# Both 1024-row matrices times M3 by seven products of half blocks; table rows stored unsplit; the adapters' chunks in another order

## The chip, the cores and the metric

One Trainium2 chip; the kernel uses one of its NeuronCores. The metric is the device time of a run in microseconds. The time before is 886.78 us, the median of 3 runs (886.35 to 887.19).

## The reference, cut to what matters

`x` is 64 x 64 x 1024: 4096 rows of 1024 numbers, 32 tiles of 128 rows, two batches of 64 rows to a tile. Four residual layers follow one another:

```
x = x + base0(x) + 2 * sum_e gate[e] * (x A0[e]^T) B0[e]^T   # 1024x1024 weight, router over 8 experts, rank 16, top 2
x = x + W1[condition[b]]^T x[b]                              # mixes the 64 rows of a batch
x = x + (x B2[id]^T) A2[id]^T                                # 64 second adapters, rank 16, one per batch
x = x + x W3^T + b3 + 2 * (x A3[id]) B3[id]                  # 1024x1024 weight, 32 third adapters, rank 16
```

Everything is float32. The kernel multiplies the weight matrices with each other first. With M0 = I + W0^T and M3 = I + W3^T it makes M0 M3, B0 M3, U2 M3 (U2: all 64 second adapters' output matrices as 1024 rows), and M0 and B0 times the second adapters' 1024 and the third adapters' 512 input columns. A tile then needs one pass over these products. Each float32 product is made as three matmuls of a rounded part (`_hi`) and a rest (`_lo`): hi x hi, lo x hi, hi x lo (`PASSES`).

## The kernel before

**Setup** is a list of groups, `GROUPS`, of a chunk (512 columns of the right-hand side, in `mov`) and a block (128 rows of the left-hand side, in `stat`). A group is 8 x 3 = 24 matmuls into one of four banks (`product`, L1484). There are 27 groups of the three chunks with adapters' columns (chunks 0 and 1: second adapters; chunk 2: third adapters; blocks: eight of M0 and B0) and 34 of the two chunks of M3 (eight blocks of U2, B0, eight of M0): 61 groups, 1464 matmuls of 512 columns. A block is loaded by SyncE three groups ahead, gets its piece of the identity from GpSimd (`stat_identity`), its rounded part from ScalarE (`stat_hi`) and its rest from VectorE (`stat_lo`, L1094 is the helper `rest`). The next chunk is loaded and split one piece a group. Each group's result is evicted by ScalarE (`group_hi`) and VectorE (`group_lo`) as rounded part and rest. Those of the D chunks go to a stage in memory of the core and from there to the tables `t2` and `t3` in DRAM (`store_md`), whose rows hold rounded part, rest and the adapter's own matrix, 416 columns. Those of U2 go to the table `tu2` (`store_u2`), those of M0 M3 stay as weights: the plain columns in `w`, and B11, B21, B22 and the sums T1 to T4 for the products of the tiles.

**The tiles** are worked in 16 pairs (`fore`, `step`, `last`); for each pair a 1024 x 832 part of the product is already made by seven products P1 to P7 of half blocks, from the pair's rows and their sums (`sums`, on GpSimd). For each tile SyncE loads the chosen table rows (`load_md`), GpSimd puts them into `w` and `b03` (`place_w`, L707, two casts; `place_b`), ScalarE and GpSimd split the adapters' own matrices (`ud_hi`, `ud_lo`), and TensorE makes the plain product (`plain`, L1513), the hidden product (L1562), the gate's transpose, the experts (L1528), the mixing (L1534) and the ranks (L1556). Each engine's order is written out by hand; engines wait for each other by semaphores. All DMAs are issued by SyncE on one queue, in program order. The load for the next tile waits until GpSimd has placed the one before.

The time of the seam matters here: in the kernel before, `store_md` of the last D chunk lies some 30 groups ahead of the first `load_md`.

## Time and profile before

| | |
|---|---|
| median of 3 runs | 886.78 us |
| span of the profiled execution (the profile gives no time of its own beside it) | 884.5 us |
| TensorE busy | 876.8 us, 99% |
| VectorE busy | 651.4 us, 74% |
| ScalarE busy | 350.5 us, 40% |
| GpSimd busy | 241.3 us, 27% |
| DMA | 187.71 MB, 212 GB/s |

Busy time counts an instruction from its start to its end. Matmuls overlap, so the rate of TensorE is read from the starts in the chain, not from the mean length. A line such as L1094 is a helper's: operations are told apart by the names of what they write.

### The profile page before, as it was taken

The numbers are of one execution on the slowest core, as the hardware profiler recorded it, in microseconds if no ns is written. First come the engines' busy times: TensorE is split into PE (matmuls) and PEld (weight loads), VectorE is DVE, ScalarE is ACT, GpSimd is POOL, SyncE is SP. The second block draws the span as 40 slices with busy tenths as digits, with TensorE's granted clock in tenths as the row PEclk, the third lists the DMA queues.
The fourth block names the chain that finished last, engine by engine and source line by source line (L and its number), as shares of the span: only waits on it lengthen the run. The fifth ranks groups of instructions, "written<-read, shape, count | busy, mean of one in ns | idle before, by whom it ended". The sixth has DMA issues, their size and how long they took to land.

```text
span 884.5 us, 15284 instructions
## 1 busy us (share of the span) xinstructions
PE 876.8 (99%) x4668; PEld 810.8 (92%) x4668; DVE 651.4 (74%) x1865; ACT 350.5 (40%) x800; POOL 241.3 (27%) x379
## 2 busy tenths in 40 slices
PE   8999999999999999999999999999999999999997
PEld 7888888888888889999999999999999999999997
DVE  6555444444358634798998899898899899899896
ACT  5544333333334423434434434434334344345333
POOL 1100010010000004415415425325325335235230
PEclk9999999999999999999999999999999999999999
DMA  7978686899663575566666667667667667566674
GB/s 243 311 265 282 207 262 211 284 350 274 191 193 126 162 222 174 164 179 200 213 185 216 202 182 230 196 188 222 192 188 230 185 195 224 186 195 215 196 205 144
DMA packets 105606, 187.71 MB, mean 212 GB/s; under 512 B 20022, under 2 KB 66870, under 8 KB 105526
## 3 DMA queue, kind: packets, MB, share of 16 engines
q1 hardware_dynamic: 105526, 186.76, 68.3%
q8 instruction: 37, 0.61, 0.3%
q14 instruction: 43, 0.35, 0.1%
HBM read 143.20 MB, written 49.81 MB: 218 GB/s over the span
## 4 chain that ended last, share of the span: by engine, by line
PE 96%; DMA 1%; DVE 1%; POOL 1%; SPq 0%; issue 0%; ACT 0%; DVEq 0%; POOLq 0%
PE ps_o L1487 28%; PE ps_w L1521 16%; PE ps_d L1513 15%; PE ps_d L1521 12%; PE ps_s L1487 9%; PE ps_o L1534 5%; PE ps_d L1528 4%; PE ps_o L1556 3%; PE ps_s L1562 1%; PE ps_w L1528 1%; DMA chunk_a_raw<-mov 1%; DMA stat_raw<-x 1%; PE ps_s L1568 0%; PE ps_o L1589 0%; DVE outb L1333 0%
## 5 line engine op out<-in xcount | busy, mean ns | idle before, releaser
L1094 DVE TENSOR_TENSOR stat_lo<-stat_raw,stat_hi 128x1024 fp32r<-128x1024 f32 (+1 forms) x127 | 152.2, 1199 | 22.2 <-ACT stat_hi L798 19.8
L798 ACT ACTIVATE stat_hi<-stat_raw 128x1024 fp32r<-128x1024 f32 (+1 forms) x127 | 116.7, 931 | 12.1 <-POOL stat_raw L682 5.4
L1513 PE MATMUL ps_d<-w_hi,stat_hi 128*128 128x392 f32 x256 | 86.9, 340 | 0.3 <-POOL w_lo L707 0.3
L1513 PE MATMUL ps_d<-w_hi,stat_lo 128*128 128x392 f32 x256 | 86.8, 339 | 0.0
L1513 PE MATMUL ps_d<-w_lo,stat_hi 128*128 128x392 f32 x256 | 86.8, 339 | 0.0
L1487 PE MATMUL ps_o<-chunk_a_hi,stat_hi 128*128 128x512 f32 x216 | 84.3, 390 | 0.9 <-DVE chunk_a_lo L1094 0.9
L1487 PE MATMUL ps_o<-chunk_a_lo,stat_hi 128*128 128x512 f32 x216 | 84.1, 389 | 0.0
L1487 PE MATMUL ps_o<-chunk_a_hi,stat_lo 128*128 128x512 f32 x216 | 84.0, 389 | 0.0
L707 POOL CAST w_hi<-mdraw 128x512 fp32r<-128x512 f32 x32 | 31.3, 977 | 157.0 <-DMA mdraw<-t 156.9
L682 POOL TENSOR_TENSOR stat_raw<-stat_raw,ident 128x128 f32<-128x128 f32 x40 | 20.5, 514 | 186.5 <-DMA stat_raw<-stat 186.5
L1487 PE MATMUL ps_o<-chunk_b_hi,stat_hi 128*128 128x512 f32 x152 | 59.1, 389 | 0.0
L1487 PE MATMUL ps_o<-chunk_b_hi,stat_lo 128*128 128x512 f32 x152 | 59.1, 389 | 0.0
L1487 PE MATMUL ps_o<-chunk_b_lo,stat_hi 128*128 128x512 f32 x152 | 59.1, 389 | 0.0
L1487 PEld LDWEIGHTS ps_o<-chunk_a_hi,stat_hi 128*128 128x128 f32 x216 | 40.5, 188 | 9.9 <-DVE chunk_a_lo L1094 1.5
L1513 PEld LDWEIGHTS ps_d<-w_hi,stat_hi 128*128 128x128 f32 x256 | 48.0, 188 | 0.7 <-issue 0.6
L1487 PEld LDWEIGHTS ps_o<-chunk_a_lo,stat_hi 128*128 128x128 f32 x216 | 40.5, 188 | 8.5
L1487 PEld LDWEIGHTS ps_o<-chunk_a_hi,stat_lo 128*128 128x128 f32 x216 | 40.6, 188 | 8.3
L1513 PEld LDWEIGHTS ps_d<-w_hi,stat_lo 128*128 128x128 f32 x256 | 48.0, 188 | 0.1
L798 ACT ACTIVATE y_hi<-y_raw 128x416 fp32r<-128x416 f32 x48 | 26.4, 550 | 54.8 <-DVE y_raw L1362 48.3
L1513 PEld LDWEIGHTS ps_d<-w_lo,stat_hi 128*128 128x128 f32 x256 | 48.0, 188 | 0.0
L743 POOL TENSOR_TENSOR rows_raw<-rows_raw,stat_raw 128x512 f32<-128x512 f32 x32 | 46.4, 1451 | 2.3
L1521 PE MATMUL ps_w<-T_hi,stat_hi 128*128 128x416 f32 x128 | 46.4, 363 | 0.1
(230 smaller groups left out, 2346.4 us busy)
## 6 DMA issues: line engine op xcount, KB each, us to landing
up<-tu SPq DMA_DIRECT2D x124, 256.0 KB, 4.6
stat_raw<-stat SPq DMA_DIRECT2D x59, 512.0 KB, 4.2
mdraw<-t SPq DMA_DIRECT2D x128, 208.0 KB, 3.2
stat_raw<-x SPq DMA_DIRECT2D x32, 512.0 KB, 3.4
out<-outb SPq DMA_DIRECT2D x30, 512.0 KB, 5.5
t<-md_a SPq DMA_DIRECT2D x16, 576.0 KB, 5.4
rows_raw<-x SPq DMA_DIRECT2D x32, 256.0 KB, 3.7
chunk_a_raw<-mov SPq DMA_DIRECT2D x24, 256.0 KB, 5.5
```

Source lines behind the costliest of these rows:

```text
L682: nc.gpsimd.tensor_tensor(out=raw[:, s, :], in0=raw[:, s, :], in1=ident[:, :], op=ALU.add).then_inc(pool_stat, 1)
L707: last = nc.gpsimd.tensor_copy(w[part][:, :, MD_AT:P_AT].rearrange("p k (q r) -> p k q r", r=RANK), rows.rearrange("p q (k r) -> p k q r", ...
L743: nc.gpsimd.tensor_tensor(out=dst, in0=in0, in1=in1, op=op).then_inc(pool_s, 1)
L798: return nc.scalar.activation(dst, src, ACT.Copy)
L1094: return nc.vector.tensor_tensor(out=dst, in0=src, in1=rounded.bitcast(F32), op=ALU.subtract)
L1487: last = nc.tensor.matmul(ps_g[g % BANKS][:, :], st[g % RING][a][:, k, :], mchunk[c % 2][v][:, k, :], start=k == 0 and m == 0, stop=k == K ...
L1513: last = nc.tensor.matmul(plain_bank(t)[:, 0:WCOLS], rows[a][:, k, :], w[c][:, k, :], start=k == 0 and m == 0, stop=k == KB - 1 and m == l ...
L1521: last = nc.tensor.matmul(ps[:, 0:SH], rows[a][:, k, :], weights[c][:, k, :], start=first and k == 0 and m == 0, stop=k == HALF_KB - 1 and ...
L1528: last = nc.tensor.matmul(ps, hgT[t % 2][a][:, :], b03[c][:, cols], start=first and m == 0, stop=m == len(PASSES) - 1, skip_group_check=True)
L1534: last = nc.tensor.matmul(out_bank(turn, n)[:, 0:OW[n]], mix[turn % 2][a][:, :], y[t % 2][c][:, Y[n]], start=first and m == 0, stop=m == l ...
L1556: return nc.tensor.matmul(out_bank(turn, n)[:, OK[n]], stackT[:, :], up[:, OX[n]], start=first, stop=True, skip_group_check=True)
L1562: last = nc.tensor.matmul(ps_ud, d3m[:, k, :, :, :].rearrange("p h b r -> p (h b r)"), u2s[:, k, :, :, :].rearrange("p h b r -> p (h b r)" ...
```

## The change

- The 27 D groups come in the order chunk 2, 0, 1. The first chunk (third adapters) is worked at the start; chunks 0 and 1 (second adapters) at the end of setup.
- Between them, M0 and U2 times M3 are made in 8 units (`unit`), each two blocks (s and s+4) by all 1024 columns, with seven products of 12 matmuls and sums of half blocks, of quarters of M3 and of outputs. The order in a unit is P1, P5, P6, P3, P7, P2, P4, in three banks, with two sets of banks. B0 times M3 stays at 48 matmuls.
- The sums of M3's quarters and their splits are made beside the first chunk (`m3_lo`, `m3_hi`, `m3_t3`, at groups 3, 4, 6 and 7).
- The tables' rows are stored in float32, unsplit: B0's 16 columns by a DMA of their own (`store_mb`), 272 columns a row. `place_w` and `place_b` make rounded part and rest from them: a cast and a subtraction on GpSimd.
- The first pair has an order of its own (`first`): P1 and P2 ahead of the first plain product, P6 ahead of the second.
- T1 to T4 are made of unsplit sums in four operations and split at the end of setup (`t_sum`, `final_hi`, `final_lo`). Several semaphores are merged.

The diff, cut to its core:

```diff
-    GROUPS = [(c, s) for c in D_CHUNKS for s in M0_FIRST + [B0_BLOCK]]
-    GROUPS += [(3, s) for s in U2_BLOCKS + [B0_BLOCK] + M0_BLOCKS]
-    GROUPS += [(4, s) for s in M0_BY_TWO + U2_BLOCKS + [B0_BLOCK]]
+    GROUPS = [(c, s) for c in (2, 0, 1) for s in M0_FIRST + [B0_BLOCK]]
+    PREPARED = {3: 0, 4: 1, 6: 2, 7: 3}
...
+            def m3_lo(k):
+                dve.wait_ge(pool_m3, m3_adds(k))
+                dve.wait_ge(ld_m3[k], 64)
+                subtract(CT1raw[:, k, :], CT4raw[:, k, :], C3raw[:, k, :]).then_inc(dve_m3sum, 1)
+                dve.wait_ge(dve_m3sum, 4 * k + 1)
+                subtract(CT2raw[:, k, :], CT3raw[:, k, :], CT1raw[:, k, :]).then_inc(dve_m3sum, 1)
+                dve.wait_ge(act_m3, PRODUCTS * k + 4)
+                rest(CB22[lo][:, k, :], CT3raw[:, k, :], CB22[hi][:, k, :]).then_inc(dve_m3sum, 1)
+                rest(CB11[lo][:, k, :], C3raw[:, k, :], CB11[hi][:, k, :])
+                dve.wait_ge(dve_m3sum, 4 * k + 2)
+                rest(CT1[lo][:, k, :], CT1raw[:, k, :], CT1[hi][:, k, :])
+                dve.wait_ge(pool_t3, k + 1)
+                subtract(CT4raw[:, k, :], C3raw[:, HALF_KB + k, :], CT2raw[:, k, :]).then_inc(dve_m3sum, 1)
...
+            for g in range(EACH):
+                if g + 2 < EACH:
                     stat_lo(g + 2)
+                if g in PREPARED:
+                    m3_lo(PREPARED[g])
+            a_sums(0)
+            for which in range(PRODUCTS):
+                a_lo(0, which)
+
+            def unit(u):
+                more, rows = u + 1 < UNITS, u >= M0_UNITS
+                if not more:
+                    stat_lo(B0_NUMBER)
+                out_sum(u, C12)
+                if rows:
+                    row_lo(u, C12)
+                out_sum(u, C22)
+                if more:
+                    a_sums(u + 1)
+                    a_lo(u + 1, A11_AT)
+                    a_lo(u + 1, S1_AT)
+                if rows:
+                    row_lo(u, C22)
+                out_sum(u, C11)
...
+            def quarter(ps, rows, weights, first):
+                for k in range(HALF_KB):
+                    for m, (a, v) in enumerate(PASSES):
+                        last = nc.tensor.matmul(ps[:, :], rows[a][:, k, :], weights[v][:, k, :], start=first and k == 0 and m == 0,
...
+                quarter(W, a_parts(u, A11_AT), CB11, True).then_inc(pe_prod, 1)
+                pe.wait_ge(dve_a, done(u, P5))
...
+                quarter(Y, a_parts(u, S1_AT), CT1, True).then_inc(pe_prod, 1)
+                pe.wait_ge(dve_a, done(u, P6))
+                pe.wait_ge(act_wpart, 3 * u + 1)
+                quarter(W, a_parts(u, S2_AT), CT2, False).then_inc(pe_prod, 1)
...
+                pe.wait_ge(dve_csum, summed(u, C22))
+                quarter(W, a_parts(u, A22_AT), CT4, False).then_inc(pe_prod, 1)
...
+            def store_mb(c):
+                sp.wait_ge(act_ev, made(c))
+                table, first = table_rows(c)
+                sp.dma_start(table[first:first + PER, :, B0_COLS].rearrange("a p f -> p a f"), md_b0[c][:, :, :]).then_inc(st_mb, 16)
...
+                if g == G - 1:
+                    for n in range(STORES):
+                        store_md(1, n)
+
+            sp.wait_ge(ld_ids, 16 * 4)
+            choose(0)
             choose(1)
+            store_mb(1)
+            load_s2(0)
+            for made_c in D_CHUNKS:
+                sp.wait_ge(st_md[made_c], 16 * STORES)
+            sp.wait_ge(st_own, 16 * OWN_STORES)
+            load_md_first(slice(0, MAIN_COLS.stop), ld_md)
             load_s3(0)
             load_s4(0)
+            sp.wait_ge(st_mb, 16 * len(D_CHUNKS))
+            load_md_first(B0_COLS, ld_mb)
...
+                rows = mdraw[:, :, MAIN_COLS].rearrange("p q (k r) -> p k q r", r=RANK)
+                upper_w, lower_w = [v[:, :, MD_AT:P_AT].rearrange("p k (q r) -> p k q r", r=RANK) for v in w]
+                nc.gpsimd.tensor_copy(upper_w, rows).then_inc(pool_md, 1)
+                pool.wait_ge(pool_md, 2 * t + 1)
+                nc.gpsimd.tensor_tensor(out=lower_w, in0=rows, in1=upper_w.bitcast(F32), op=ALU.subtract).then_inc(pool_md, 1)
...
+            def first():
+                a, b = 0, 1
+                pe.wait_ge(dve_x0, 1)
+                pe.wait_ge(dve_final, 4 + len(FINALS))
+                pe.wait_ge(dve_set, SETS)
+                pe.wait_ge(act_ev, G)
+                winograd(ps_w, A11, B11, True).then_inc(pe_p[0], 1)
+                pe.wait_ge(dve_b0, 1)
+                winograd(ps_x, A12, B21, True).then_inc(pe_p[1], 1)
+                pe.wait_ge(act_b0, 2)
+                pe.wait_ge(pool_md, 2 * a + 2)
+                plain(a, range(KB)).then_inc(pe_hl, 1)
+                hidden_product(a)
+                pe.wait_ge(act_part, 1)
+                pe.wait_ge(dve_s, s_order(0).index(1) + 1)
+                winograd(ps_w, S[1], T2, False).then_inc(pe_p[5], 1)
+                pe.wait_ge(dve_x1, 1)
+                pe.wait_ge(pool_md, 2 * b + 2)
+                plain(b, range(KB)).then_inc(pe_hl, 1)
```

## Rows read from the trace of the kernel before

**Rows 1.** The page: its first line and the busy times.
```profile
span 884.5 us, 15284 instructions
PE 876.8 (99%) x4668; PEld 810.8 (92%) x4668; DVE 651.4 (74%) x1865; ACT 350.5 (40%) x800; POOL 241.3 (27%) x379
```

**Rows 2.** Waits of TensorE: for whom, us in total, times, longest.
```profile
PE ps_w L1482 <- POOL ident L665: 1.5, 1, 1.5
PE ps_o L1487 <- DVE chunk_a_lo L1094: 0.9, 1, 0.9
...
PE ps_d L1513 <- POOL w_lo L707: 0.3, 1, 0.3
```

**Rows 3.** Chain that ended last, setup: start, length in us, what.
```profile
29.96 16.32 PE ps_o L1487 x72
...
329.16 5.45 PE ps_s L1487 x24
```

**Rows 4.** Stretches: us, each engine's busy us, granted clock, DMA share, GB/s.
```profile
9.16:57.20 48.04, 48.04 (x211) 39.63 (x212) 31.50 (x44) 24.93 (x39) 5.54 (x10) 1.00 0.81 280
155.00:247.00 92.00, 92.00 (x408) 76.17 (x407) 39.48 (x51) 32.37 (x51) 7.87 (x17) 1.00 0.89 275
449.00:817.00 368.00, 367.91 (x2171) 363.37 (x2171) 332.93 (x1141) 149.83 (x405) 148.92 (x220) 1.00 0.67 203
880.00:884.50 4.50, 0.48 (x3) 0.14 (x2) 1.81 (x4) 0.00 (x0) 0.00 (x0) 0.83 0.64 233
```

**Rows 5.** Groups by form: count, busy us, mean ns, idle before.
```profile
L1094 DVE TENSOR_TENSOR rows_lo<-rows_raw,rows_hi 128x512 fp32r<-128x512 f32 x40 | 27.6, 689 | 18.9 <-ACT rows_hi L798 18.4
L743 POOL TENSOR_TENSOR stat_raw<-stat_raw 128x512 f32<-128x512 f32 x32 | 41.6, 1300 | 4.9 <-DMA stat_raw<-x 3.5 <-PE ps_o L1487 1.4
```

**Rows 6.** VectorE in order of time, setup and loop: start, length in us.
```profile
28.91 0.69 DVE L1094 TENSOR_TENSOR rows_lo<-rows_raw,rows_hi 128x512 fp32r<-128x512 f32 x1
29.52 0.68 DVE L1094 TENSOR_TENSOR md_a<-ps_o,md_a 128x512 fp32r<-128x512 f32 x1
30.12 1.22 DVE L1094 TENSOR_TENSOR stat_lo<-stat_raw,stat_hi 128x1024 fp32r<-128x1024 f32 x1
...
541.34 2.31 DVE L1094 TENSOR_TENSOR stat_lo<-stat_raw,stat_hi 128x1024 fp32r<-128x1024 f32 x1
```

**Rows 7.** TensorE in order of time, the warm-up, early and late.
```profile
2.12 1.70 PE L1482 MATMUL ps_w<-ident 128*128 128x128 f32 x7
...
4.68 2.00 PE L1482 MATMUL ps_w<-ident 128*128 128x128 f32 x12
```

**Rows 8.** DMA packets of two stretches: 215 to 216 us, 212.5 to 213.
```profile
DMA packets 664, 0.34 MB, mean 339 GB/s; under 512 B 1, under 2 KB 664, under 8 KB 664
...
DMA packets 488, 0.10 MB, mean 194 GB/s; under 512 B 385, under 2 KB 479, under 8 KB 488
```

**Rows 9.** SyncE in order of time: DMA issues of 1024 packets each.
```profile
207.90 2.50 SPq L587 DMA_DIRECT2D w_raw<-wr  x1
...
212.26 0.57 SPq L448 DMA_DIRECT2D t<-u2k  x1
```

**Rows 10.** The page's DMA issues: count, KB each, median us to landing.
```profile
mdraw<-t SPq DMA_DIRECT2D x128, 208.0 KB, 3.2
```

**Rows 11.** GpSimd in order of time, the second tile's rest of a pair.
```profile
544.07 0.61 POOL L707 CAST w_lo<-mdraw 128x512 fp32r<-128x512 f32 x1
```

**Rows 12.** Chain that ended last, first pair and a later one.
```profile
354.24 2.27 PE ps_w L1521 x12
...
357.43 0.44 PE ps_s L1562 x8
...
360.21 1.14 PE ps_d L1521 x6
...
548.48 4.26 PE ps_d L1513 x24
```

More of the change, by code:

```diff
@@ L387, in build, with summed @@
         pe_out = [sem(f"pe_out{n}") for n in range(3)]
+        C12, C22, C11, C21 = range(4)
+        def summed(u, which):
+            return 3 * u + which + 1
         CONSTS = 6
@@ new lines, in load_a @@
+            def load_a(u, at):
+                n = u * PRODUCTS + at
+                if n >= SPOTS:
+                    sp.wait_ge(pe_prod, n - SPOTS + 1)
+                else:
+                    sp.wait_ge(pe_group, max(g for g in range(EACH) if g % RING == spot(u, at) // 2) + 1)
+                if u > 0 and at in (A11_AT, A12_AT, A22_AT):
+                    sp.wait_ge(ld_a[at], 16 * u)
+                first = (M0_BLOCKS if u < M0_UNITS else U2_BLOCKS)[0] + u % HALF_KB
+                block = first if at in (A11_AT, S4_AT, A12_AT) else first + HALF_KB
+                columns = upper if at in (A11_AT, S1_AT) else lower
+                sp.dma_start(araw(u, at), stat[block][:, columns, :]).then_inc(ld_a[at], 16)
@@ L656, in last @@
                 sp.wait_ge(st_last, 16 * 6)
-            pairs(step)
+            pairs(first, step)
             last(PAIRS - 1)
@@ L790, in last @@
                 mix_identity(TURN_A)
-            pairs(step)
+            pairs(first, step)
             last(PAIRS - 1)
@@ L1086, in last @@
                 h3T_last(TURN_A)
-            pairs(step)
+            pairs(first, step)
             last(PAIRS - 1)
@@ new lines, in _ @@
+            for u in range(UNITS):
+                unit(u)
+            b0_upper, b0_lower = [[v[:, half, :] for v in st[B0_NUMBER % RING]] for half in (upper, lower)]
+            pe.wait_ge(dve_stat, stats(B0_NUMBER))
+            pe.wait_ge(dve_row, 4 * (UNITS - 2 - M0_UNITS) + C21 + 1)
+            quarter(ps_u[0][0], b0_upper, CB11, True).then_inc(pe_b0, 1)
+            pe.wait_ge(dve_csum, summed(UNITS - 2, C11))
+            quarter(ps_u[0][1], b0_upper, CT1, True).then_inc(pe_b0, 1)
+            pe.wait_ge(act_b0, 1)
```

1454 lines of the change are left out of this document (928 added, 526 removed).

## The prediction

> **What bounds the kernel now.** I read the page first: TensorE is busy for 876.8 of 884.5 us, VectorE for 651.4 [rows 1]. Then the waits of TensorE: the longest are 1.5 us before the warm-up, 0.9 us for the first chunk and 0.3 us at the first tile [rows 2]. Third, the chain that ended last: from 9.16 us on it is one unbroken series of matmuls, three groups of 24 in 16.32 us, a fourth in 5.45, that is 0.2267 us from matmul to matmul and 5.44 us a group of 512 columns (the mean of 389 ns a matmul overlaps the next one and must not be summed) [rows 3]. So a setup matmul that is left out is worth 0.2267 us exactly as long as nothing else is late. Last, the stretches: in setup VectorE is busy 43 to 66% and the DMA engines 81 to 89%, in the loop over tiles VectorE 90% [rows 4]. There is room, but the question of this case is latency at the seams, and there are two new ones.
>
> **Part 1, the products.** Before, both 1024-row matrices times M3 take 16 blocks x 2 chunks x 24 = 768 matmuls. After, 8 units of 7 products of 12 make 672. The 48 of B0 and the 648 with the adapters' chunks stay. 96 x 0.2267 = **21.8 us removed**.
>
> **Part 2, inside a unit (19.04 us, a product 2.72).** VectorE makes 4 sums and 7 low parts, in the units of the second adapters also 3 outputs and 4 low parts: 18 operations of 0.6 us from start to start (0.69 each) [rows 5, 6], about 12 us. The tight order is at the end: the output C22 waits for product 5 (13.6 us into the unit), then come 4 sums, each on the one before, at 0.73, and one low part: 13.8 + 0.6 + 2.9 + 0.7 = 18.0, and the next unit wants it at 19.04. ScalarE copies the first product out of its bank some 4 us into the next unit, wanted at 5.44. Loads are issued a product or more ahead; 22 issues at 0.47 make 10 of 19 us on the queue. I take 0; bounds 0 and 1 us in each of 7 units. B0 and the chunk after it: eight chunk pieces are loaded two products ahead and split during B0's 10.9 us, 0.
>
> **Part 3, the seam into the units.** While the first chunk is used (nine groups, it ends at 57.2), VectorE gets 4 preparations of M3, 10 operations each, beside the splits of the stationary blocks. The sixth block can be split from about 26.3 to 27.4 (its load waits for group 1, ScalarE first evicts group 2, which ends at 24.5). Then: 4 x 6.7 (10 starts at 0.6 plus two dependent steps and the wait on GpSimd's 1.3 us subtraction), 3 splits of 1024 columns at 1.14, four dependent sums 2.9, one low part 0.7: 27.4 + 26.8 + 3.4 + 3.6 = about 61.4 to 61.8. TensorE stands for **4.6 us**. From below: 2 if the first preparation slips ahead. From above: a VectorE operation beside GpSimd's stretches (2.31 against 1.23 us for 1024 columns) [rows 6]; of each preparation 1.3 us lie beside GpSimd, half of it lost: +0.65 x 4 = 2.6, so 7.2.
> A wait this long may let the clock fall. At the very end, after its last matmul at about 880.3, the granted clock of the stretch is 0.83 [rows 4], so it fell from 2.4 to 1.2 GHz within 4.2 us of idling, and in the warm-up 7 matmuls took 1.70 us and later 12 took 2.00 [rows 7]. If the first product behind the wait runs at half, it costs 2.7; I take **0.9** between 0 and 2.7. The Trainium skill, "TensorE: Matmul & The Clock Gate", Part 1, has the same two levels and says that an idle array falls back to the lower; by that rule the whole product is paid and the sum is 1.8 us worse.
>
> **Part 4, the seam into the tiles.** Before, the second adapters' and third adapters' tables lay in memory long before; the first tile's rows were loaded inside setup and TensorE waited 0.3 us. Now the last chunk of setup is the second adapters', so its table is stored, loaded and split after the last group. With T the end of that group:
> - The stores of 2 MB wait for the eviction of the last group but one (T-4.7), 8 issues at 0.47. 4096 packets of 512 B; a stretch that is nothing but such packets moved 664 in 1 us [rows 8], so 6.2 us: drained at T+2.7.
> - The 16 columns of B0 go as 4096 packets of 64 B, behind them in the queue, after T+0.8. Small packets: 488 in 0.5 us, 385 of them under 512 B [rows 8], so 16 engines handle them in 16 ns or less; 4096 take 2.9 to 4.2 us. The issue itself can block: 1024 packets of 32 B held the queue's issuer for 2.50 us where 1024 of 512 B held it for 0.57 [rows 9]. T+5.7.
> - x's half block and four loads of 128 KB, 2 us, and the rest of the landing: T+9 (a table row takes 3.2 us from issue to landing, median) [rows 10].
> - GpSimd: a cast and now a subtraction of 512 columns, 0.6 + 1.3 [rows 5, 11]: placed at T+11.
> - Then, in GpSimd's order, two sums 2.6, two small splits 1.5, B0's columns 0.5; only then may the second tile's four loads be issued (1.9) and land (2.8), and be placed (1.9): T+22.2.
> Until the second tile's plain product TensorE has P1, P2, the plain product, the hidden product and P6: 2.27 + 2.27 + 4.26 + 0.44 + 2.27 = 11.5 us [rows 12]. **10.7 us** idle; a lower clock in the first wait is swallowed by the second. Bounds: 7 (packets and landings at their best) and 21 (below).
> - Behind it only P7, the experts and the hidden product stand before T1 (3.7 us, before also P6: 6.0 from 354.24 to 360.21) [rows 12], and the exponential of the second gate is now queued behind the eviction that waits for the experts. Experts at +2.9, exponential +3.3, rest of the gate 1.8, low part 0.4: +5.7. **2.0 us**, bounds 0 and 3. The 0.3 of before goes.
> The Trainium skill, "DMA: Bandwidth & Descriptors", Specifications, speaks against this edit: below 512 B a transfer is a read-modify-write and off line rate. The 32 B packets of the trace went faster by the packet than the 512 B ones, but they went into SBUF; no row shows 64 B written to memory. What slow small packets would do here is rival D, priced from rows.
>
> **Part 5, the loop over tiles.** A table row shrinks from 208 to 136 KB. On GpSimd the cast of the low part (0.6) becomes a subtraction (1.3), 0.8 us a tile with B0's, 32 times, 25 us on an engine that is busy 40%. Hidden: the second tile's place ends at 544.7, the product that wants it starts at 548.48, 3.8 us later [rows 11, 12]. The next on that queue, ScalarE's h2, moves by 0.8 where VectorE takes it up 1.1 us later. 0; if the cover were gone 0.3 x 15 pairs. 27 low parts of D groups leave VectorE in setup, off the path. The merged semaphores cost 0.
>
> **Sum.** -21.8 + 4.6 + 0.9 + 10.7 + 2.0 - 0.3 = -3.9 us: span 880.6. The page gives the profiled execution's span only, 884.5; the median 886.78 lies 2.3 above, so 882.9; I forecast **883.1 us**, 0.4% less.
>
> **Rivals.** (B) The seams are shorter: first wait 2, no clock loss, last seam 7, gate 0: -21.8 + 9 - 0.3 = -13; I price it half way, 877. For it: each bound was stacked on a worst order. Against: the chain of part 4 has ten steps that can't overlap.
> (C) VectorE and GpSimd hinder each other in the preparation of M3, and the clock's product is paid whole: +2.6 + 1.8: 887.5, no change. For it: the 2.31 us row.
> (D) Slower: the 64 B packets decide. Place: the queue between the second adapters' table and the first tile. Price: at the issuer's pace of [rows 9], 2.50 us for 1024, the store takes 10.0 us in place of 2.9, +7.1; the same store in unit 0 (behind it the sixth block of unit 1, and in ScalarE's order behind that the first product's bank) adds 2: 892.2. It turns the sign from a store of 7 us on (+3.9) and shows as slower from 8.4 us. For it: the issuer's row. Against: the mixed stretch of [rows 8], and that the issuer may only have waited for room.
> (E) The last 1 us of a unit isn't there: each unit is late by 1, 7 us: 890. Against: 0.6 a start is the most regular row.
> That the change would not leave matmuls out is no rival: the count is written in its loops.
>
> **How the numbers follow.** Forecast 0.42 (its own range 880 to 886), B 0.20, C 0.14, D 0.14, E 0.10. A change within 0.2%, 1.8 us, can't be told from none. Faster: B and most of the forecast's case, 0.56. Same: 0.04 of the forecast, C, together 0.17. Slower: D, E and a tail of the forecast's, 0.27. Range 876.5 to 891: it leaves out the far end of B and the upper part of D.
>
> **What would show it.** Of the matmuls of 128x512, 1368 instead of 1464. Idle TensorE in three places: before the first product of unit 0 (4 to 6 us, released by VectorE's low part), before the first plain product and before the second (5 and 5, GpSimd's w_lo), before T1 of the first pair (2, VectorE's y_lo). No waits at all in units 1 to 7 and in the later pairs. Wrong if TensorE waits inside the units, if the loop over tiles gets longer than 33.5 us a pair, or if the store of B0's columns takes over 6 us.

## The result, and the profile after

The changed kernel takes 907.44 us (median of 4 runs, 905.93 to 908.36), the kernel before 886.57 beside it (4 runs): ratio 1.0232, 95% interval 1.0218 to 1.0247. It is 2.3% slower. The forecast was 883.1 us and its range ended at 891.

The page's first line and busy times [answers to rows 1]:

```profile
span 905.7 us, 15339 instructions
PE 867.2 (96%) x4572; PEld 797.5 (88%) x4572; DVE 682.5 (75%) x1896; ACT 368.2 (41%) x827; POOL 289.5 (32%) x379
```

TensorE has 96 matmuls less, as written, and is busy 9.6 us less; the span is 21.2 us longer. Waits of TensorE (whom for, us in total, times, longest) [rows 2]:

```profile
PE ps_d L2073 <- POOL w_lo L919: 14.2, 2, 10.1
PE ps_d L2006 <- DVE stat_lo L1461: 8.0, 1, 8.0
PE ps_s L1984 <- DVE stat_lo L1461: 2.7, 1, 2.7
...
PE ps_d L2081 <- DVE y_lo L1461: 1.8, 1, 1.8
...
PE ps_o L2006 <- ACT wpart L1026: 1.4, 1, 1.4
```

I cut both traces at three marks, read from TensorE in order of time. T is the end of the last matmul of the last group of setup (0.2 to 0.5 us behind the start of what follows, since matmuls overlap).

| stage, us | before | after | difference | forecast |
|---|---|---|---|---|
| start to T | 340.0 | 334.6 | -5.5 | -16.3 |
| T to the third tile's plain product | 29.0 | 49.7 | +20.8 | +12.4 |
| from there to the end | 515.5 | 521.4 | +5.9 | 0 |
| span | 884.5 | 905.7 | +21.2 | -3.9 |

So the forecast missed 10.8 us in setup, 8.4 at the seam into the tiles and 5.9 in the loop. The next lines show where.

**Setup.** Stretches (us, busy us of PE, PEld, DVE, ACT, POOL, granted clock, DMA share, GB/s) behind TensorE's wait of 2.7 us, of the wait before unit 0, and of unit 0's first 6 us [rows 4]:

```profile
48.60:53.40 4.80, 4.80 (x14) 3.80 (x15) 4.76 (x6) 2.45 (x5) 1.68 (x2) 0.64 0.04 13
61.40:69.40 8.00, 0.00 (x1) 0.03 (x1) 7.72 (x12) 4.08 (x8) 3.23 (x4) 0.64 0.19 66
69.40:72.50 3.10, 3.10 (x7) 2.45 (x8) 3.10 (x6) 1.96 (x4) 0.00 (x0) 0.50 0.00 0
72.50:75.50 3.00, 3.00 (x12) 2.38 (x11) 0.36 (x1) 1.01 (x2) 0.00 (x0) 0.78 0.03 4
```

In the wait TensorE does nothing and VectorE is busy 7.72 of 8.00 us: this is VectorE's wait. Behind it the clock is at its lower level for 3.1 us, and unit 0 takes 21.2 us from start to start where units 2 to 7 take 19.04. The clock fell behind the wait of 2.7 us that ends at 48.58 too: the group of 24 matmuls there takes 7.2 us instead of 5.44. Setup as a whole loses nothing by that, for unit 0 waits for VectorE and would only have waited longer, as in a_order. VectorE and GpSimd in a preparation of M3 [rows 6]:

```profile
32.16 0.68 DVE L1461 TENSOR_TENSOR C_lo<-C_raw,C_hi 128x512 fp32r<-128x512 f32 x1
32.76 1.78 DVE L1461 TENSOR_TENSOR CT_lo<-CT_raw,CT_hi 128x512 fp32r<-128x512 f32 x1
34.46 0.81 DVE L1476 TENSOR_TENSOR CT_raw<-C_raw,CT_raw 128x512 f32<-128x512 f32 x1
```
```profile
32.31 1.68 POOL L887 TENSOR_TENSOR CT_raw<-CT_raw 128x512 f32<-128x512 f32 x1 [1.23 <-DVE CB_lo L1461]
```

An operation that takes 0.68 us takes 1.78 beside GpSimd's `m3_t3`. That ends at 33.99, VectorE's 0.55 us later, at 34.54: as if VectorE's work began only then.

**The seam into the tiles.** The chain that ended last, from the last store of the table to the first tile's rows (start, us, what):

```profile
333.87 0.58 SPq L557
334.46 0.06 issue
334.51 0.87 SPq L591
...
339.96 0.15 SPq L591
...
340.22 0.37 SPq L563
...
344.85 3.19 DMA mdraw<-t
348.04 0.05 issue
348.09 0.62 POOL w_hi L917
```

L591 is the read of a table number into a register of SyncE (`choose`), 0.5 to 1.2 us each, eight for the first two tiles: 5.7 us between the stores of the table and the store of B0's columns (L563), with the whole queue behind it. Before, the first tile's loads were issued inside setup, at 289.4 us, and nothing waited for them. The last store of the second adapters' table had been issued at 201.0 us, so 88 us or 16 groups lay between the two, not the 30 groups that I gave ahead of the prediction. SyncE in order of time after that:

```profile
340.22 0.37 SPq L563 DMA_DIRECT2D t<-md_b  x1
340.63 2.27 SPq L663 DMA_DIRECT2D stat_raw<-x  x1
343.25 0.90 SPq L609 DMA_DIRECT2D mdraw<-t  x2
```

The packets of 342 to 345 us, most of them the 64 B ones [rows 8]:

```profile
DMA packets 2908, 0.51 MB, mean 171 GB/s; under 512 B 2702, under 2 KB 2780, under 8 KB 2908
```

The store is issued at 340.2; its packets run from 341 to 344 us, and the issue behind it (L663) takes 2.27 us. The first plain product starts at T+15.6, the second at T+28.6 (forecast T+22.2).

**The loop.** VectorE and GpSimd of one pair, in order of time [rows 11]:

```profile
492.06 1.29 POOL L919 TENSOR_TENSOR w_lo<-mdraw,w_hi 128x512 fp32r<-128x512 f32 x1
492.07 1.32 DVE L1784 TENSOR_TENSOR spare_f<-spare_f 32x32 f32<-32x32 f32 x1
```

VectorE's operation of 32x32 numbers (the last of `hidden_sum`) lasts as long as GpSimd's subtraction. Alone it takes 0.18 us. The gate stands behind it. The kernel before had the same in small, beside the cast of [rows 11], which ends at 544.68:

```profile
544.21 0.51 DVE L1304 TENSOR_TENSOR spare_f<-spare_f 32x32 f32<-32x32 f32 x1
```

Pairs of tiles, from plain product to plain product, are 33.53 us long before; after, the second to fourth take 33.05 to 33.54, and of the eleven behind them two 33.5 and nine 34.0 to 34.4. The trace says which pairs are the long ones. From the third pair on the two instructions start within 0.02 us of each other. In all four pairs of 33.53 or 33.54 VectorE's takes 0.18 us and GpSimd's 1.34 to 1.35, as if VectorE's had got in first; in all nine long ones VectorE's takes 1.32 and GpSimd's 1.29. One of the four, the pair from 417.3 us:

```profile
425.00 1.35 POOL L919 TENSOR_TENSOR w_lo<-mdraw,w_hi 128x512 fp32r<-128x512 f32 x1
425.00 0.18 DVE L1784 TENSOR_TENSOR spare_f<-spare_f 32x32 f32<-32x32 f32 x1
```

### The profile page after: what moved, and what is told of

Same layout as the page of the kernel before. It is cut to its first block, busy times and chain, and to the rows that moved or that the text cites. A ratio compares the mean times of both kernels' runs of the same rounds, so it can differ in the third digit from the quotient of the medians.

```text
span 905.7 us, 15339 instructions
## 1 busy us (share of the span) xinstructions
PE 867.2 (96%) x4572; PEld 797.5 (88%) x4572; DVE 682.5 (75%) x1896; ACT 368.2 (41%) x827; POOL 289.5 (32%) x379
## 4 chain that ended last, share of the span: by engine, by line
PE 68%; DVE 21%; issue 5%; DMA 2%; SPq 2%; POOL 1%; ACT 1%; DVEq 0%; ACTq 0%; POOLq 0%
PE ps_w L2081 13%; PE ps_d L2006 10%; PE ps_d L2081 9%; PE ps_o L1984 9%; PE ps_o L2006 8%; PE ps_d L2073 5%; DVE stat_lo L1461 4%; PE ps_d L2088 4%; PE ps_o L2094 3%; PE ps_s L1984 2%; DVE CT_lo L1461 2%; DVE spare_f L1760 1%; DVE outb L1813 1%; DVE spare_f L1759 1%; DVE y_lo L1461 1%
## 5 line engine op out<-in xcount | busy, mean ns | idle before, releaser
L1461 DVE TENSOR_TENSOR stat_lo<-stat_raw,stat_hi 128x512 fp32r<-128x512 f32 (+1 forms) x150 | 149.4, 1014 | 67.0 <-ACT stat_hi L1026 48.0
L1026 ACT ACTIVATE stat_hi<-stat_raw 128x512 fp32r<-128x512 f32 (+1 forms) x150 | 115.5, 789 | 82.7 <-DVE stat_raw L1479 41.0
L1984 PE MATMUL ps_o<-chunk_hi,stat_hi 128*128 128x512 f32 x168 | 65.6, 391 | 0.6 <-DVE chunk_lo L1461 0.6
L1984 PE MATMUL ps_o<-chunk_lo,stat_hi 128*128 128x512 f32 x168 | 65.4, 389 | 0.0
L1984 PE MATMUL ps_o<-chunk_hi,stat_lo 128*128 128x512 f32 x168 | 65.4, 389 | 0.0
L2073 PEld LDWEIGHTS ps_d<-w_hi,stat_hi 128*128 128x128 f32 x256 | 49.1, 192 | 14.8 <-issue 14.8
L1026 ACT ACTIVATE rows_hi<-rows_raw 128x512 fp32r<-128x512 f32 x52 | 32.6, 627 | 58.3 <-DMA rows_raw<-u 27.3
L1461 DVE TENSOR_TENSOR rows_lo<-rows_raw,rows_hi 128x512 fp32r<-128x512 f32 x52 | 36.0, 694 | 20.5 <-ACT rows_hi L1026 20.0
L2081 PE MATMUL ps_w<-T_lo,stat_hi 128*128 128x416 f32 x128 | 44.9, 351 | 0.0
L2081 PE MATMUL ps_w<-T_hi,stat_lo 128*128 128x416 f32 x128 | 44.9, 351 | 0.0
L1813 DVE TENSOR_TENSOR outb<-ps_o,bias_row 128x416 f32<-128x416 f32 (+1 forms) x93 | 41.9, 506 | 1.2 <-issue 0.3
```

The costliest lines, as they stand in the source:

```text
L1026: return nc.scalar.activation(dst, src, ACT.Copy)
L1461: return nc.vector.tensor_tensor(out=dst, in0=src, in1=rounded.bitcast(F32), op=ALU.subtract)
L1813: nc.vector.tensor_tensor(out=dst[:, OX[n]], in0=out_bank(turn, n)[:, OK[n]], in1=bias_row[:, OX[n]], op=ALU.add).then_inc(dve_out[n], 1)
L1984: last = nc.tensor.matmul(ps_g[g % BANKS][:, :], st[n % RING][a][:, k, :], mchunk[c][v][:, k, :], start=k == 0 and m == 0, stop=k == KB - ...
L2073: last = nc.tensor.matmul(plain_bank(t)[:, 0:WCOLS], rows[a][:, k, :], w[c][:, k, :], start=k == 0 and m == 0, stop=k == KB - 1 and m == l ...
L2081: last = nc.tensor.matmul(ps[:, 0:SH], rows[a][:, k, :], weights[c][:, k, :], start=first and k == 0 and m == 0, stop=k == HALF_KB - 1 and ...
```

## The experiments

Thirteen kernels are the changed one with an edit (a_), three the kernel before with an edit (b_); a row of the table is each one's profiled execution. Ratios are to runs of the kernel before on the same chip. Edits are cut to their core: the counts of semaphores that follow from them are left out.

| run | unit 0 | T | first plain | second | third | from the third to the end | ratio (interval) |
|---|---|---|---|---|---|---|---|
| before | | 340.0 | T-0.2 | T+9.6 | T+29.0 | 515.5 | |
| after | 69.4 | 334.6 | T+15.6 | T+28.6 | T+49.7 | 521.4 | 1.0232 (1.0218 to 1.0247) |
| b_again | | 340.3 | T-0.2 | T+10.3 | T+29.7 | 515.3 | 1.0019 (1.0004 to 1.0033) |
| b_sum | | 340.2 | T-0.2 | T+10.4 | T+29.7 | 518.5 | 1.0043 (1.0026 to 1.0059) |
| b_sub | | 340.2 | T-0.2 | T+11.1 | T+30.4 | 524.8 | 1.0106 (1.0077 to 1.0135) |
| a_cast | 69.7 | 334.5 | T+15.3 | T+29.1 | T+50.2 | 514.8 | 1.0150 (1.0125 to 1.0175) |
| a_cut | 69.9 | 334.4 | T+16.7 | T+29.8 | T+53.1 | 516.1 | 1.0192 (1.0169 to 1.0215) |
| a_early | 70.3 | 336.2 | T+12.8 | T+25.6 | T+46.8 | 523.2 | 1.0245 (1.0223 to 1.0267) |
| a_early2 | 69.7 | 335.3 | T+12.7 | T+26.0 | T+47.1 | 521.7 | 1.0214 (1.0193 to 1.0236) |
| a_early2_mb | 70.4 | 336.0 | T+10.3 | T+25.4 | T+47.0 | 522.8 | 1.0207 (1.0184 to 1.0230) |
| a_seam | 70.0 | 335.7 | T+12.6 | T+21.7 | T+41.3 | 523.1 | 1.0156 (1.0132 to 1.0179) |
| a_t3 | 68.4 | 334.2 | T+16.4 | T+29.2 | T+50.3 | 524.0 | 1.0255 (1.0238 to 1.0272) |
| a_order | 68.2 | 333.6 | T+16.2 | T+28.8 | T+50.0 | 523.2 | 1.0235 (1.0217 to 1.0252) |
| a_prep | 65.8 | 331.7 | T+15.8 | T+28.5 | T+50.7 | 522.8 | 1.0211 (1.0188 to 1.0233) |
| a_fill | 68.7 | 331.2 | T+18.7 | T+32.9 | T+52.5 | 523.2 | 1.0278 (1.0261 to 1.0295) |
| a_all | 66.6 | 331.3 | T+11.1 | T+26.9 | T+47.5 | 516.7 | 1.0092 (1.0072 to 1.0113) |
| a_best | 65.0 | 331.0 | T+11.1 | T+26.3 | T+45.9 | 517.6 | 1.0090 (1.0059 to 1.0122) |
| a_best2 | 65.7 | 329.8 | T+14.3 | T+24.3 | T+44.9 | 516.2 | 1.0055 (1.0037 to 1.0073) |

How far a column moves by itself can be read from kernels that don't touch its stage. Unit 0 starts at 69.4 to 70.4 us in the changed kernel and the six with the same setup ahead of it (a_cast, a_cut, a_early, a_early2, a_early2_mb, a_seam). The loop takes 521.4 to 524.0 us in the changed kernel and the eight with its loop (a_early, a_early2, a_early2_mb, a_seam, a_t3, a_order, a_prep, a_fill), depending on how many pairs are 33.53.

### The loop: GpSimd's subtraction

**b_again**, the kernel before:

```diff
+                pool.wait_ge(pool_md, 2 * t + 1)
+                nc.gpsimd.tensor_copy(dst, rows).then_inc(pool_md, 1)   # the cast of the low part once more
```

> The kernel before, with the cast of the low part made twice, so that GpSimd works 0.6 us longer a tile as with the subtraction, by one-input operations alone. Theory (two-input operations hold VectorE up): pairs stay at 33.53 or gain under 0.15 us. Rival 1 (GpSimd's queue is late): pairs grow to 34.1 to 34.4, as in the changed kernel.

Measured: pairs of 33.53 us (one of 33.73), the loop 515.3. GpSimd is 0.6 us later a tile and in the loop nobody waits for that; rival 1 is out. Only the first plain product of the second tile waits 0.7 us more for its rows (T+10.3).

**b_sum**, the kernel before:

```diff
-                        last = nc.gpsimd.tensor_copy(dst, rows)
+                        last = nc.gpsimd.tensor_tensor(out=dst, in0=rows.bitcast(F32), in1=rows.bitcast(F32), op=ALU.add)
```

> The kernel before, with one GpSimd instruction of each tile exchanged: the low part of a table row's 512 columns is written by a two-input operation (the stored low part added to itself, so it comes out doubled) instead of a cast. The repeated cast left the pairs of tiles at 33.53 us. Theory (two-input operations on GpSimd and VectorE's operations on SBUF hold each other up): pairs of 34.0 to 34.4 here, 5 to 9 us over the loop, 893 to 896, with setup as before. Rival (the loop's loss comes from the smaller rows or the other order of the memory, and the subtraction only adds to it): pairs of 33.53, 887.

Measured: pairs of 33.68 us for most, the loop 3 us longer, 1.3 of them in one pair of 34.85 in which TensorE waits 1.0 us for ScalarE. The direction is the theory's, the 0.15 us a pair are a third of its least: a miss for both.

**b_sub**, the kernel before:

```diff
+                nc.gpsimd.tensor_tensor(out=dst[lo], in0=rows[lo].bitcast(F32), in1=dst[hi].bitcast(F32), op=ALU.subtract).then_inc(pool_md, 1)
```

> The kernel before, with the low part of a table row written on GpSimd as the changed kernel does it: a subtraction of the upper part just placed, behind a wait for it, from what was loaded (here the stored low part, so the output takes low minus upper). The sum of the low part with itself took 1.03 us and made the pairs of tiles 33.68; the repeated cast left 33.53. Theory (VectorE's operation on two SBUF inputs waits for the GpSimd instruction in progress, beyond a slack of some 0.9 us TensorE waits too): GpSimd's operation takes 1.29, VectorE's beside it 1.3, pairs of 34.0 to 34.3, the total 892 to 895. Rival (the changed kernel's other edits make its loop longer): pairs of 33.7 again.

Measured: of fourteen pairs behind the first nine of 34.0 to 34.1, one of 34.3, three of 34.6 to 35.1 and one of 33.53. In the last VectorE's operation took 0.18 us; it did so too in one of 34.73, where TensorE waited 0.9 us for ScalarE. The loop is 9.3 us longer, 1.1% on the whole. The exchange of one cast, with the wait for the upper part that b_again has too, is enough to lose more than the changed kernel's loop does.

**a_cast**:

```diff
-                nc.gpsimd.tensor_tensor(out=lower_w, in0=rows, in1=upper_w.bitcast(F32), op=ALU.subtract).then_inc(pool_md, 1)
+                nc.gpsimd.tensor_copy(lower_w, rows).then_inc(pool_md, 1)
```

> The changed kernel, with the low parts of the table rows and of B0's columns written by a cast instead of the subtraction (so they repeat the upper part; the true rest is left out). Theory (GpSimd's subtraction costs the loop 0.7 us a pair): pairs back at 33.53, the loop 6 us shorter, the seam into the tiles 1 to 2 us shorter: 899 to 901. Rival (the loop is longer for another reason): 905 to 907, only the seam's 1 to 2 us.

Measured: pairs of 33.51 to 33.66 from the third on, the loop 6.6 us shorter. The theory holds. The seam's 1 to 2 us did not come.

**a_cut**:

```diff
+                for n in range(4):
+                    last = nc.gpsimd.tensor_tensor(out=lower_w[:, 2 * n:2 * n + 2], in0=rows[:, 2 * n:2 * n + 2], in1=..., op=ALU.subtract)
```

> The changed kernel, with GpSimd's subtraction for the low part of a table row in four instructions of 128 columns instead of one of 512 (1.29 us). Seen so far: VectorE's operation on two SBUF inputs beside it ends when GpSimd's ends, at 0.6, 1.0 and 1.3 us, and the pair of tiles is 33.5, 33.7 and 34.1 to 34.3 long. Theory (a VectorE operation waits for the GpSimd instruction that is in progress): it waits for 0.35 us instead of up to 1.3, the pairs come back to 33.5 to 33.7, the total to 898 to 902. Rival (GpSimd's whole stretch counts, not its instruction): the pairs stay at 34.1 or grow, 907 or more.

Measured: pairs of 33.5 to 33.8, the loop 5.3 us shorter, though GpSimd's four pieces take 1.7 us instead of 1.3. The total (profiled 903.6) gained 2.1 only, because the third tile came 3.4 us later behind T; why is open (see a_seam).

The same two operations in five kernels, start and length: b_again, b_sum, b_sub, a_cast, a_cut.

```profile
545.29 0.61 POOL L708 CAST w_lo<-mdraw 128x512 fp32r<-128x512 f32 x1
545.43 0.51 DVE L1306 TENSOR_TENSOR spare_f<-spare_f 32x32 f32<-32x32 f32 x1
545.97 0.62 POOL L711 CAST w_lo<-mdraw 128x512 fp32r<-128x512 f32 x1
```
```profile
612.73 1.03 POOL L711 TENSOR_TENSOR w_lo<-mdraw 128x512 fp32r<-128x512 f32 x1
612.86 0.95 DVE L1307 TENSOR_TENSOR spare_f<-spare_f 32x32 f32<-32x32 f32 x1
```
```profile
719.58 1.29 POOL L709 TENSOR_TENSOR w_lo<-mdraw,w_hi 128x512 fp32r<-128x512 f32 x1
719.59 1.33 DVE L1304 TENSOR_TENSOR spare_f<-spare_f 32x32 f32<-32x32 f32 x1
```
```profile
626.58 0.62 POOL L919 CAST w_lo<-mdraw 128x512 fp32r<-128x512 f32 x1
626.60 0.63 DVE L1784 TENSOR_TENSOR spare_f<-spare_f 32x32 f32<-32x32 f32 x1
```
```profile
629.82 1.73 POOL L920 TENSOR_TENSOR w_lo<-mdraw,w_hi 128x128 fp32r<-128x128 f32 x4
629.82 0.50 DVE L1787 TENSOR_TENSOR spare_f<-spare_f 32x32 f32<-32x32 f32 x1
```

In these traces VectorE's operation ends 0.03 to 0.05 us behind the GpSimd instruction that was in progress, whatever its kind: a cast holds it up too (b_again: both end at 545.9, the second cast starts behind; a_cut: the first piece ends at 630.28, VectorE's operation at 630.32). What counts is the length of the single instruction: 0.6 us is hidden, 1.0 costs a pair 0.15, 1.3 costs 0.5 and more; and it costs nothing where VectorE's operation gets in first, as the pairs of 33.53 in the changed kernel show. The Trainium skill, "SBUF — State Buffer", "SBUF: two separate sides", has this rule: VectorE and GpSimd share a pair of ports, and whoever starts first holds it for its whole instruction, against a VectorE operation with two inputs in SBUF. The traces agree to 0.05 us.

### The seam into the tiles

**a_early**: `choose(0)` and `choose(1)` moved from behind the last group to the second group of chunk 0.

```diff
+                if g == EACH + 1:
+                    sp.wait_ge(ld_ids, 16 * 4)
+                    choose(0)
+                    choose(1)
```

> The changed kernel, with the table numbers of the first two tiles read into SyncE's registers during the third adapters' chunk's second group instead of behind the last group. Theory (the 5.7 us of register reads delay the store of B0's columns, the loads and all behind them): the first plain product 3 to 5.7 us earlier (the drain of the stores, T+2.7, then ends last), the total 902 to 904. Rival (the stores of 2 MB or GpSimd's order end the wait anyway): under 1.5 us.

(The place is in chunk 0, of second adapters, and not in the third adapters' chunk, as this says.)

Measured: 2.8 us earlier behind T, the second plain product 3.0; but T itself is 1.6 later, half of it behind the new place: the reads (245.7 to 251.8 us) held up loads of blocks, and two groups waited 1.0 us together. No gain in total.

**a_early2**: the same at `g == FINAL_FIRST + 3`, the fourth group of the last chunk.

> The changed kernel, with the table numbers of the first two tiles read into SyncE's registers in the middle of the last chunk of setup, where the queue issues nothing for longer. Theory (the register reads hold up the chain from the last group to the first tile, and the earlier place cost 1.6 us because loads stood behind it): the last group ends as in the changed kernel, the first plain product 12.8 us behind it instead of 15.6, the second 25.6 instead of 28.6: 3 us less. Rival (the gain is only borrowed from the next wait): the second plain product stays 28.6 behind.

Measured: 2.9 and 2.6 us earlier behind T. T is 0.8 later, all of it from ahead of the edit's place (the units end 0.8 later). The third plain product keeps the gain. In total 1.4 us less (906.04 against 907.44), and the two intervals overlap.

**a_early2_mb**:

```diff
-            store_mb(1)
             load_s2(0)
...
             load_md_first(slice(0, MAIN_COLS.stop), ld_md)
+            store_mb(1)
```

> As the run with the register reads in the middle of the last chunk, and the store of B0's 4096 pieces of 64 B issued behind the first tile's loads of the main columns instead of ahead of them. Theory (64 B packets cost 3 us of a shared queue, beside stores that drain anyway): the first plain product 0 to 2 us earlier, the second as before or 1 us later, total within 2 us of the other run. Rival (the packets of 64 B are what the loads wait for): both plain products 3 us or more earlier.

Measured: first plain product 2.4 us earlier, the second 0.6, the third 0.1. The 64 B packets cost the first product 2.4 us and the rest nothing: GpSimd's order ends the second wait.

**a_seam**: on a_early2.

```diff
                 place_w(0)
+                ud_lo(0)
+                place_b(0)
                 (the sums into Sraw[2] and Sraw[3])
-                ud_lo(0)
-                place_b(0)
@@ ScalarE
                 ud_hi(0)
+                b03_hi_all()
+                gate_exp(0)
                 s_hi(0, 2)
                 s_hi(0, 3)
-                b03_hi_all()
-                ud_hi(1)
-                gate_exp(0)
                 after_P6(0)
+                ud_hi(1)
@@ VectorE
+                gate(0)
                 hidden_sum(0)
-                gate(0)
```

> The run with the register reads in the last chunk (first plain product T+12.6, second T+26), with three pieces of the order at the first tile exchanged: on GpSimd the small splits and B0's columns ahead of the last two sums of x's blocks, on ScalarE the first gate's exponential ahead of the second tile's small split, on VectorE the first gate ahead of the hidden sum. Theory (the second tile's rows come late because GpSimd's two sums, 2.6 us, stand before what frees the buffer; and the exponential behind a wait for the second tile's loads delays the experts and with them the third tile's rows): second plain product at T+22.5 to 24, the third 33.5 to 34.5 behind the first, 901 to 903. Rival (loads and landing set it): T+25 or more.

Measured: second plain product at T+21.7, 4.3 us earlier; third at T+41.3, 5.8 earlier; ratio 1.0156 against 1.0214. The first pair, 28.7 us, is shorter than either expectation. GpSimd of this run:

```profile
348.10 0.74 POOL L938 TENSOR_TENSOR u2s<-mdraw,u2s 128x256 fp32r<-128x256 f32 x1
...
349.46 0.25 POOL L930 CAST b_hi<-mdraw 128x64 fp32r<-128x64 f32 x1
349.79 0.32 POOL L932 TENSOR_TENSOR b_lo<-mdraw,b_hi 128x64 fp32r<-128x64 f32 x1
```

and of the changed kernel, same operations:

```profile
352.47 1.72 POOL L937 TENSOR_TENSOR u2s<-mdraw,u2s 128x256 fp32r<-128x256 f32 x1
...
355.29 1.23 POOL L929 CAST b_hi<-mdraw 128x64 fp32r<-128x64 f32 x1
```

Besides the two sums of 1.25 us, the old order had GpSimd itself held up by VectorE's long low parts (0.74 became 1.72, 0.25 became 1.23). They hold each other up both ways. So `b_lo` ends at T+14.4 instead of a_early2's T+19.0, and that is the second product's gain. The gate waited for its exponential, in ScalarE's order behind the second tile's loads, 3.4 us in the changed kernel and 4.6 in a_all, and 1.8 here. Three engines' orders changed at once here, and what each gives behind the second product was not separated. Nor does this wait explain the first pairs of 36.4 to 36.6 us in a_cut, a_early2_mb and a_all against 34.1: in a_cut it was 2.3, shorter than in the changed kernel. That stays open.

### The first seam

**a_t3**:

```diff
-                if g in PREPARED:
-                    m3_t3(PREPARED[g])
@@ VectorE, m3_lo
+                subtract(CT3raw[:, k, :], CT3raw[:, k, :], CT4raw[:, k, :]).then_inc(pool_t3, 1)
```

> The changed kernel, with the difference CT3 of each preparation of M3 (4 of 128x512) made by VectorE instead of GpSimd. Theory (GpSimd's two-input operation of 1.7 us holds up VectorE's beside it, CT's low part takes 1.8 instead of 0.7): VectorE has 4 x 0.6 more to do and 4 x 1.1 less to wait, the wait for GpSimd goes too: the wait before unit 0 falls from 8 to 5 to 6.5 us, the total by 2 to 3. Rival (VectorE is only long of work): the wait grows by 2.4 to 10 us.

Measured: the wait is 6.6 us, just outside what the theory gave, and unit 0 starts 1.0 us earlier. The total isn't 2 to 3 us shorter but 2.8 longer in the profiled execution (908.5): the loop took 2.6 us more, which is within what it moves by itself. VectorE's operations are freed; the first of these lines is of the changed kernel, the second of this one:

```profile
L1461 DVE TENSOR_TENSOR CT_lo<-CT_raw,CT_hi 128x512 fp32r<-128x512 f32 x16 | 15.7, 1002 | 0.4
```
```profile
L1459 DVE TENSOR_TENSOR CT_lo<-CT_raw,CT_hi 128x512 fp32r<-128x512 f32 x16 | 11.2, 723 | 0.4
```

The 4.5 us won go largely to the four operations added (2.9).

**a_order**: M3's loads by counts instead of three a group.

```diff
+                counts = (4, 0, 3, 3, 3, 3, 0, 0, 0)
```

> The changed kernel, with the 16 pieces of M3 issued 4, 0, 3, 3, 3, 3 behind the loads of the fourth to the ninth stationary block, instead of 3 behind each of the first five and one behind the sixth. Theory (the sixth block's load waits behind M3's pieces, 6.2 us from issue to landing, and starts the whole preparation 2.7 us late): it lands 1.5 us or more earlier, TensorE's wait of 2.7 us at 48.6 shrinks under 1.5, the wait before unit 0 by 1 to 2.5. Rival (VectorE's total work sets the end, not its start): the 2.7 may go, unit 0 starts no earlier than 69 us.

Measured: the wait of 2.7 us at 48.6 shrinks to 0.5, unit 0 starts at 68.2, 1.2 earlier, and the wait before it is 9.7, not shorter: between theory and rival, and nothing in the total. The first seam is one sum of waits, set by VectorE.

**a_prep**:

```diff
-    PREPARED = {3: 0, 4: 1, 6: 2, 7: 3}
+    PREPARED = {2: 0, 4: 1, 6: 2, 7: 3}
+                counts = (4, 0, 4, 4, 4, 0, 0, 0, 0)
```

> The changed kernel, with the first of the four preparations of M3 one block earlier in every engine's order, and its loads issued 4, 0, 4, 4, 4 behind those of the stationary blocks. VectorE works without a break of 0.2 us from 30.08 to 69.26 us in the changed kernel, 39.2 us, behind 4.05 us of idling. Theory (unit 0 starts when this unbroken work ends, however the loads come): the work starts at 25 to 27, unit 0 at 65 to 67 instead of 69.4, TensorE's wait 5 to 7 in one or two places. Rival (only the last loads or GpSimd's identities set the end): unit 0 at 68 or later, as with the other order of loads.

Measured: VectorE starts the preparation at 25.24 instead of 30.08, unit 0 starts at 65.8, 3.6 us earlier, and T is 2.8 earlier. The theory holds: VectorE's unbroken work is the length of this seam. In the span only 0.5 is left, because the first pair took 1.0 and the loop 1.4 us longer (of the later pairs only the last is 33.53, the one in which VectorE's operation took 0.18 us). What decides which of the two gets in first is not settled.

**a_fill**: products of the identity in the three waits.

```diff
+            for _ in range(42):
+                nc.tensor.matmul(ps_w[:, 0:P], ident[:, :], ident[:, :], start=True, stop=True)
```

> The changed kernel, with products of the identity into an unused bank in the waits: 42 before unit 0, 60 between the second and the plain product of the first tile, 32 before the second tile's plain product. Theory (TensorE's clock falls in the waits and the work behind them pays): unit 0 in 19.04 us instead of 21.4, the second tile's plain product 4.3 instead of 6.1, together 4 us: 903. Rival (something else is late behind the waits too, so the gain is lost in the next wait): the first part, 2.4, holds, the second goes into the wait for the rest: 905 or more.

Measured: units and B0 take 164.6 us instead of 167.2. Behind the wait:

```profile
68.70:71.80 3.10, 3.09 (x14) 2.58 (x15) 3.10 (x6) 2.06 (x5) 0.00 (x0) 1.00 0.02 5
71.80:74.80 3.00, 3.00 (x15) 2.49 (x14) 0.38 (x1) 1.40 (x3) 0.00 (x0) 1.00 0.27 87
```

Unit 0 takes 19.1 us instead of 21.2: 2.1 us of it was clock. The other 0.5 is a shorter wait for ScalarE in unit 1 (0.9 instead of 1.4). At the second seam I put in too many: one is 0.22 us, not 0.17, so 60 ended at 349.9 although the rows were placed at 347.2, and 32 at 364.1 against 360.7. So the longer total says nothing of the theory; the second tile's plain product did start at full clock.

### All together

**a_all**: a_early2_mb, a_t3, a_order, a_cut and fewer products of the identity (30, 24, 20).

> The changed kernel with all the edits at once: register reads early, store of B0's columns behind the first loads, M3's pieces issued 4, 0, 3, 3, 3, 3, the difference CT3 on VectorE, the subtraction of the rows in four, and products of the identity in the three waits (30, 24 and 20, of 0.22 us). If the causes add: setup 1 to 2 (order and CT3) and 2.4 (clock) shorter, the seam into the tiles 3 (registers), 1.8 (clock) and 0 to 2 (store), the loop 4 to 6: 890 to 895, still above the kernel before, since the wait before unit 0 (5) and the store, load and place of the last table (18 to 20) stay. If they hide each other: 898 to 903.

Measured: 1.0092, the median 896.3, profiled 895.6: just above the upper end of what adding up gives, 895.

**a_best**: a_all with a_prep's order of loads and preparations, and a_seam's orders (20, 24, 10).

> All edits together: register reads in the last chunk, B0's store behind the first loads, the first preparation of M3 earlier with its loads, the difference CT3 on VectorE, the subtraction in four, the order at the first tile of the run before, and products of the identity in the three waits (20, 24, 10). If the causes add: all but the last three edits of the former combination gave 896.3; the earlier preparation 1 to 3 less, the order 4 to 6 less: 888 to 891, one or two tenths of a per cent above the kernel before. If VectorE's and GpSimd's work only moves the waits: 893 to 896.

Measured: no gain on a_all. The second plain product stays at T+26.3: GpSimd, with `place_b(0)` now ahead of the sums, waited 2.9 us for B0's columns, which a_early2_mb's order brings late. Behind that the split of the sum for P6 came late too (TensorE waited 4.2 us), and ten products of the identity ended 1.0 us after the rows were placed. Two edits, each of which had brought a plain product forward, worked against each other.

**a_best2**: without the later store.

> The former combination without the later store of B0's columns (and 6 products of the identity in the last wait instead of 10). In the former one, GpSimd, which now places B0's columns ahead of the two sums, waited 2.9 us for their landing, so the two edits worked against each other: the second plain product came 26.3 us behind the last group, against 21.7 where only the order was changed. Theory: the first plain product at T+12.6 (from T+11.1), the second at T+21.7 to 22.5, the total 891 to 893. Rival (the second tile's rows wait for something else): second at T+26, 896.

Measured: 1.0055 (1.0037 to 1.0073), profiled 890.9: 14.8 us less than the changed kernel, still 6.4 more than the kernel before. The median, 892.9, is within what was expected, the marks are not: T+14.3 and T+24.3 instead of T+12.6 and 21.7 to 22.5. The issue behind the store of B0's columns took 4.7 us here (3.9 in a_seam). Its waits of TensorE:

```profile
PE ps_d L2081 <- POOL w_lo L920: 3.4, 1, 3.4
PE ps_d L2012 <- DVE stat_lo L1464: 3.2, 1, 3.2
PE ps_o L2012 <- ACT wpart L1029: 2.1, 1, 2.1
PE ps_d L2089 <- DVE y_lo L1464: 1.8, 1, 1.8
```

To these come the products of the identity (20, 24 and 6 of 0.22 us: 11 us) that fill waits which are still there. What is left is, as I read the chain, the structure: the last table must be stored, loaded and placed behind the last group. No run removes that.

## Why the prediction was wrong

Three steps failed: part 3, which counted nothing for VectorE and GpSimd holding each other up in the preparations; part 4, which left out SyncE's register reads and GpSimd's chain beside VectorE; and part 5, which put the longer GpSimd instruction at 0. Setup, the seam and the loop came out 10.8, 8.4 and 5.9 us over the forecast.

- **Part 1** (21.8 us removed, as many matmuls less) and **part 2** (0 inside a unit) were right: units 2 to 7 take 19.04 us each without a wait in the products, B0 10.9. Rival E is out. One small miss: unit 1's bank waited 1.4 us for ScalarE, behind the table stores in unit 0 that delayed the sixth block's load.
- **Part 3 failed in size**: unit 0 started at 69.4 us, not at 61.8. On TensorE that is 4.6 forecast against waits of 8.0 and 2.7, and 1.7 us lost to the lower clock between them. Two terms were too small. The start: the sixth block landed 6.2 us after its issue, behind M3's pieces, and VectorE began the preparations at 30.08, not 27.4 (a_order and a_prep). The duration: 4 x 6.7 was 4 x 7.8 to 8.3 (in a_t3 7.1 to 8.4), since beside `m3_t3` and the identities VectorE's operations wait for GpSimd's (a_t3). I had the row (2.31 us against 1.23), left it out of the sum and priced it as half of 1.3 us a preparation in a bound; it was 1.1 us for `m3_t3` each time, and the identities' besides. (The forecast's own terms add up to 61.2, not 61.4 to 61.8.) Unit 1, with its 1.4 us wait, took 1.7 us over its 19.04.
- **The clock** (0.9): it was 2.1 in unit 0, within the bound of 2.7. The granted clock of the wait was 0.64 and of the 3.1 us behind it 0.50. By the rule of the Trainium skill that I weighed, "TensorE: Matmul & The Clock Gate", Part 1, the sum was 1.8 worse; the trace is nearer to it (1.2 worse) than to my 0.9. The second seam cost 1.8 once more: the second tile's plain product took 6.1 instead of 4.3 us [rows 12], which I had not asked for.
- **Part 4 failed**: T+28.6 for the second plain product, not T+22.2. The first missed step is SyncE's own work between two issues: the eight register reads, 5.7 us, are in the program at that place, and I counted the DMA issues only. a_early2 gives back 2.6 at the second product; for the rest the drain of the table's stores, which a_early2_mb shows at T+4.3 instead of T+2.7, would have ended last. The second term is GpSimd's chain from the first tile's rows in place (350.0) to `b_lo` (356.9): 6.9 us against 4.6 counted (a_seam: 2.0). The gate's 2.0 for T1 was 1.8, right.
- **Part 5 failed as a step**: "Hidden: the second tile's place ends 3.8 us before the product". I asked whether GpSimd's result comes late, and it doesn't; I didn't ask whom the longer instruction keeps waiting. Its "wrong if the loop gets longer than 33.5 us a pair" came true: +5.9 us. One exchanged instruction brings as much and more in the kernel before (b_sub, +9.3), the reverse exchange takes it away (a_cast, -6.6), and within the changed kernel's loop only pairs in which VectorE was held up are long.
- **Rival D** (64 B packets, +7.1): its sign came true, its mechanism not. The packets were through in 3 us, as the forecast had them, and cost 2.4 us of the first product only. **Rival C** named the right mechanism and gave it 2.6 us, with 1.8 for the clock, in one of the three places where it acts. **Rival B** is out.

The misses all have one sign. I take the reason to be the same at both seams: I took the longest chain that I knew of, and every unlisted step can only add to it.

## What to carry to other kernels

When an instruction on GpSimd gets longer, look on VectorE for what starts beside it, not only for who needs its result; an instruction cut in four can be slower in itself and faster for the kernel. When a loop takes two lengths, compare the same instruction in a long turn and in a short one: here that shows the cause without another run. At a seam list everything in the issuing engine's program between two issues, register reads too, and put such reads where the queue is idle. An edit that leaves work out on the busy engine at the price of new seams is worth its matmuls less each seam's whole chain: here 21.8 against some 16 at the first seam, clock included, and 21 at the second.
